# Zero-column matmuls on TensorE ahead of the wait for each channel's exponentials

## What is computed

```
cos_pm = jnp.cos(phase_modulators)                # [channel, head]
for wl in range(16):
    m = cos_pm[wl][None, :, None, None]
    scores = einsum('bhqd,bhkd->bhqk', Q * m, K * m) * SCALE
    scores = scores * jnp.cos(KERR * scores * scores)
    attn = jax.nn.softmax(scores, axis=-1)
    acc += einsum('bhqk,bhkd->bhqd', attn, V) * interference_weights[wl]
x = _layernorm(x + (acc / 16) @ Wo + bo)
x = _layernorm(x + ffn(x))
```

## Time and profile before

| | us |
|---|---|
| median of 3 runs | 3671.42 (3670.53 to 3673.81) |
| the profiled execution itself | 3674.77 |
| span of that execution, first to last instruction | 3672.7 |
| ACT busy | 3476.3 (95%) |
| DVE busy | 2934.6 (80%) |
| PE busy | 2688.7 (73%) |
| mean granted TensorE clock | 0.882 of full |

### The profile page before, as it was taken

How to read it: one execution, slowest core, us unless ns; L and a number is a source line. 1 busy time by engine, 2 the same in 40 slices (tenths; PEclk the granted TensorE clock), 3 DMA queues, 4 the chain that set the end, 5 groups by cost and what they waited for, 6 DMA issues and landing times.

```text
span 3672.7 us, 50238 instructions
## 1 busy us (share of the span) xinstructions
PE 2688.7 (73%) x19639; PEld 823.7 (22%) x19639; DVE 2934.6 (80%) x3858; ACT 3476.3 (95%) x635; POOL 55.8 (2%) x206
## 2 busy tenths in 40 slices
PE   5777777777777777777777777777777777777673
PEld 2222222222222222222222222222222222222222
DVE  6788777788777788777788888788888888888787
ACT  6999999999999999999999999999999999999971
POOL 0000000000000000000000000000000000000000
PEclk7988988888889889888889898889888888988986
DMA  1000000000000000000000000000000000000000
GB/s 46 1 1 1 1 1 1 1 1 1 1 1 1 1 1 1 1 14 1 1 2 1 4 2 4 2 4 1 2 4 2 4 2 1 4 2 4 2 26 29
DMA packets 19221, 16.65 MB, mean 5 GB/s; under 512 B 4177, under 2 KB 16866, under 8 KB 18722
## 3 DMA queue, kind: packets, MB, share of 16 engines
q1 hardware_dynamic: 18130, 12.54, 1.2%
q10 hardware_dynamic: 720, 0.34, 0.0%
q0 software_dynamic: 128, 0.26, 0.0%
HBM read 7.76 MB, written 5.37 MB: 4 GB/s over the span
## 4 chain that ended last, share of the span: by engine, by line
ACT 53%; issue 27%; PE 9%; DVE 4%; ACTq 4%; DMA 0%; POOL 0%; DVEq 0%; POOLq 0%
ACT probs L597 53%; PE psum L1200 7%; ACTq L590 3%; DVE x_p L668 1%; PE psum L719 1%; DVE m_pad L770 0%; ACTq L594 0%; DVE x_p L686 0%; DVE probs L843 0%; PE psum L699 0%; DVE probs L1106 0%; DVE q_s L654 0%; DVE q_t L762 0%; ACT probs L614 0%; DVE k_s L654 0%
## 5 line engine op out<-in xcount | busy, mean ns | idle before, releaser
L597 ACT ACTIVATE probs<-s_t 128x8192 f32<-128x8192 f32 (+1 forms) x512 | 3440.8, 6807 | 69.2 <-PE psum L1200 67.6
L1200 PE MATMUL psum<-probs,v_pad 128*27 128x512 f32 x15872 | 2239.1, 691 | 578.7 <-ACT probs L597 523.0
L1200 PEld LDWEIGHTS psum<-probs,v_pad 128*27 128x27 f32 x15872 | 568.4, 119 | 1976.5 <-issue 1382.2
L668 DVE SCALAR_TENSOR_TENSOR x_p<-x_p,x_y 128x1024 f32<-128x1024 f32 x640 | 782.0, 1222 | 14.2
L1385 DVE COPY o_sb<-psum 128x512 f32<-128x512 f32 x192 | 132.7, 691 | 249.9 <-PE psum L1200 237.5
L791 DVE COPY s_t<-psum 128x2048 f32<-128x2048 f32 x130 | 297.0, 2284 | 11.2 <-PE psum L749 10.2
L770 DVE TENSOR_REDUCE m_pad<-psum 128x4 f32<-128x2048 f32 x132 | 301.6, 2286 | 3.9
L699 PE MATMUL psum<-x_p,v_pad 128*27 128x512 f32 x512 | 157.1, 696 | 190.1 <-DVE x_p L686 190.1
L761 DVE TENSOR_SCALAR v_t<-psum,b_head 128x512 f32<-128x512 f32 x33 | 24.8, 751 | 208.1 <-PE psum L719 208.1
L686 DVE SCALAR_TENSOR_TENSOR x_p<-x_p,x_2k 128x1024 f32<-128x1024 f32 x128 | 156.8, 1225 | 4.4
L1184 PE MATMUL psum<-ident,o_sb 128*128 128x128 f32 x768 | 122.1, 282 | 47.9 <-DVE weighted L1373 47.9
(11 more groups left out here) (244 smaller groups left out, 990.8 us busy)
## 6 DMA issues: line engine op xcount, KB each, us to landing
x_next_dram<-weighted SPq DMA_DIRECT2D x1, 1024.0 KB, 3.9
x_group<-x_next_dram SPq DMA_DIRECT2D x1, 1024.0 KB, 4.9
loop_memory<-in_L_attn_x_dram SPq DMA_DIRECT2D x8, 128.0 KB, 2.1
x_dram<-loop_memory SPq DMA_DIRECT2D x8, 128.0 KB, 1.8
out_dram<-loop_memory SPq DMA_DIRECT2D x8, 128.0 KB, 1.8
x_dram<-probs SPq DMA_DIRECT2D x2, 512.0 KB, 3.6
out_dram<-probs SPq DMA_DIRECT2D x2, 512.0 KB, 3.6
s_t<-in_L_ffn_ew_dram SPq DMA_DIRECT2D x3, 256.0 KB
```

Of the source, the lines that this page charges most:

```text
L597: nc.scalar.activation(probs[:, w % 2, n0:], s_t[:, p, n0:], ACT.Exp, scale=scales[w % 2]).then_inc(s["exp_done"], 1)
L668: link(nc.vector.scalar_tensor_tensor(out=x_p[:], in0=x_p[:], scalar=c, in1=x_y[:], op0=ALU.add, op1=ALU.mult))
L1200: last = nc.tensor.matmul(products_of(wg)[L * b:L * b + SLOTS * A, :], v_pad[:, p, b * T + kt, c0:c0 + SLOTS * A], probs[:, w % 2, at:at + ...
```

## The change

A helper `spin_pe` is added. In each step but steps 2 and 7 it issues 2 rounds, that is 8 matmuls, whose stationary operand is 18 columns of `v_pad` that hold zeros and whose moving operand is 512 columns of `s_t`. They write to rows of the bank that the step's product accumulates into. In the first step of a group but the last they carry start and stop flags, so that they write zeros, which the product's first matmul replaces; in the others they add zeros. The wait for `exp_done` moves behind them; the wait for `o_copied` (a bank's last contents have been copied) now stands ahead of them.

```diff
+SPINS = 2
+SPIN_STEPS = tuple(w for w in range(W) if w not in (2, 7))
...
+        def spin_pe(w, wg, p):
+
+            for r in range(SPINS if w in SPIN_STEPS else 0):
+                for b in range(NB):
+                    nc.tensor.matmul(products_of(wg)[L * b:L * b + VPAD, :], v_pad[:, p, b * T, 0:VPAD],
+                                     s_t[:, p, b * S:(b + 1) * S], start=(w in FIRST_OF and w < W - 1), stop=(w in FIRST_OF and w < W - 1))
+
...
                             for w in range(W):
                                 if w in PRODUCT_STEPS:
                                     piece_pe(pe, PRODUCT_STEPS[w], u, p)
-                                pe.wait_ge(s["exp_done"], u * W + (w + 1))
                                 if w in FIRST_OF:
 
                                     wg = FIRST_OF[w]
                                     pe.wait_ge(s["o_copied"], u * NWG + (wg + 1))
+                                spin_pe(w, wg, p)
+                                pe.wait_ge(s["exp_done"], u * W + (w + 1))
```

## The result

| | before | after |
|---|---|---|
| median, us | 3672.61 (4 runs) | 3793.03 (4 runs, 3792.14 to 3793.81) |
| ratio, 95% interval | | 1.0313 (1.0288 to 1.0338) |
| span of the profiled execution, us | 3672.7 | 3790.6 |
| mean granted TensorE clock | 0.882 | 0.938 |
| ACT waits for products, us in all (times) | 67.6 (43) | 178.2 (93) |

What follows compares the result with a forecast made beforehand. ACT, busy 95% of the span, was taken as the bound. Back edges (+5.27 us, 14 times: 73.8) and other passages (+0.99, 17 times: 16.8) gave +90.6 on 3671.4: 3762.0 us; range 3648 to 3810, the forecast's own 3710 to 3800.

Steps and rivals of the forecast that it cites:

- The gain: Ahead of step 0: step 14's product at full clock lets ACT start 1.50 us earlier at each of 31 passages.
- Step 0 behind a back edge: After PE's branch, added rounds delay step 0's product, so ACT waits at step 2: 3.07 us lost, half clock included.
- Step 4: Rounds behind the late piece delay exponential 6: 2.49 us lost with half clock, 3.70 us behind a back edge.
- Steps 8 and 11: Same order of piece and rounds costs up to 1.71 us, but ACT has room; counted as zero.
- That zero columns hold the clock: Assumption at the added rounds: matmuls of zeros raise the clock as much as a product's round does.
- The rival that they do nothing: Zero columns do not hold the clock, so 1.50 us stay lost and delays come: 3808.5 us, chance 0.08.
- Rivals 3 and 4: 3: back edge not felt, clock holds, 3649.7 us, chance 0.11; 4: only the gain, step 4 free, 3624.9 us, chance 0.09.
- rivals 1 and 2: 1: full clock everywhere, 3685.8 us, chance 0.10; 2: half clock at the back edge only, 3709.5 us, chance 0.13.
- rival 6: Whole kernel: gains and delays cancel within 0.2%, about 7 us; chance 0.07.

Runs made afterwards that it cites:

- e4: The change with all its rounds, but in steps 4, 8, 11 and 15 placed ahead of the piece's wait instead of behind it: 3674.7 us.
- e9: The change with rounds in steps 4 and 14 only, those of step 4 behind the piece's wait as in the change: 3670.2 us.
- e10: The change with rounds in steps 4 and 14 only, those of step 4 ahead of the piece's wait: 3624.2 us.
- e3: The change without its rounds in steps 0 and 15: 3742.4 us.
- e7: The change with rounds in steps 0 and 14 only: 3665.3 us.
- e8: The change with rounds in steps 14 and 15 only: 3675.1 us.
- e6: The change with rounds in step 14 alone, and one round there instead of two: 3670.0 us.
- e1: The change with its two rounds in step 14 alone: 3637.1 us.

## Why the prediction came out as it did

**The direction and the reason were right.** The forecast said slower, with new gaps of ACT ahead of step 6 in nearly all units and ahead of step 2 in every second one, and half clock behind the branch and around the piece. All of it is in the trace after: gaps ahead of step 6 in all 32 units, and ahead of step 2 in the first unit and the 14 behind a back edge. e4 and e9 with e10 show that it is the place behind the piece's wait; e3, e7 and e8 show that rounds on either side of the branch cost time. The size came out low: 3793 us lies inside the forecast's own range of 3710 to 3800, near its top, and the reason given for that top, a longer slow stretch, is a part of what happened.

**The gain** was put at 1.50 us at each of 31 passages. 24 passages have a gap of 0.25 or 0.26 us, a gain of 1.52. The 7 back edges of the second loop kept 1.47 to 1.49 us. The miss is 7 x 1.2, about 8.5 us. There the rounds behind the piece of step 11 and PE's feed-forward work in steps 12 and 13 add up until the product of step 14 starts 1.3 us late; I had set the cost of steps 8 and 11 at zero and counted feed-forward work nowhere. In e4, whose rounds in steps 8 and 11 stand ahead, all 31 gaps are 0.26 us or less. Step 14's products kept full clock, in the first loop behind 1.52 to 1.57 us of idle, as forecast; but the ground given for it, that 1.73 us had kept the clock in the rows of before, was not a safe one, since 1.66 us in the same trace had not (under e6).

**Step 0 behind a back edge** was put at 3.07 us; the gaps are 3.4 to 3.9 us. With the 0.10 us of lost overlap that is some 0.6 us more, a fifth. I took one stretch of half clock like those of the earlier trace rows, on the rounds alone. The trace after has half clock from 1635.8 to 1642.5 around the branch, twice as long: it sets in while PE idles and stays when the rounds start, so they run at half clock from their first column to their last, and the product behind them still takes 3.98 us instead of 3.64. That is about half of the 0.6 us; the rest is that PE reaches the rounds later, 10.14 us after the unit's first exponential starts (1638.43 - 1628.29) where the forecast had 9.78. The branch itself is as before (a median of 3.48 us against 3.46 in the earlier trace rows). The added 14 x 0.6 us are some 8 us. The Trainium skill (Runtime: NRT & Kernel Launch, section "Instruction fetch mechanics") says that a taken branch to code that is no longer loaded waits for a fetch by DMA. The trace fits, since the same loop's branch takes 3.3 to 3.9 us on PE when it goes back and 0.08 us when it falls through, but no run here shows the fetch as the cause.

**Step 4** was put at 2.49 us and, behind a back edge, at 3.70. Measured, with the 0.10 us of lost overlap: 3.74 behind back edges, as forecast. The others split: 2.06 to 2.29 in the first loop, 3.66 to 4.03 in the second. Of the first loop's 2.1 us, 0.8 are the rounds (e9) and the rest half clock on a part of the work (in the windows above, 1553.9 to 1557.2; the piece starts at 1554.50). In the second loop's units within an iteration the piece comes another half microsecond later, and half clock lasts twice as long. The window around the piece of such a unit (columns as above):

```profile
2458.40:2465.10 6.70, 5.38 (x28) 0.50 0.01 2
```

and the piece in PE's timeline:

```profile
2459.72 1.06 PE L701 MATMUL psum<-x_p,v_pad 128*27 128x512 f32 x2 [2.56 <-DVE x_p L688]
```

In sum the gaps ahead of step 6 grew by 96.1 us (105.0 against 8.9 before) where some 94 were forecast. That they agree so well is luck: with the lost overlap, the 8 units of the first loop are some 3 us below the forecast together, the 9 of the second some 13 above it, and the very first unit, which the forecast leaves out, has 3.6 us.

**Steps 8 and 11** were put at zero. Step 8's product costs 4 us of gaps ahead of step 10; step 11's share is in the 8.5 us above.

**That zero columns hold the clock**, which the trace of before could not show, is shown: step 14 at full clock in all units, 1.00 in its window. The rival that they do nothing (3808.5) lies close to the measured time, but its mark, products of over 5 us in step 14, is absent. By the time alone it would have been nearer than the forecast. Rivals 3 and 4, the faster ones, fall by the gaps at steps 2 and 6; rivals 1 and 2 (full clock everywhere, or at the piece) by the windows at 0.50; rival 6 by the time.

In sum, ACT's gaps after are 111 us more than before: 39 less ahead of step 0 (46.5 were forecast), 50 more ahead of step 2 (43), 96 more ahead of step 6 (94) and 4 more ahead of step 10 (none). The span grew by 118; the remaining 7 us are, for the most part, the overlap of 0.10 us that each of some 50 additional interruptions costs.

## What to carry to other kernels

Matmuls that only hold the clock belong into time in which the engine would otherwise wait, and so ahead of the wait that ends last, not merely ahead of some wait: in an in-order queue everything behind an earlier wait, or behind a branch that the engine is late from, is paid in full. Count for each place how long the engine idles behind the last instruction that it can already run; where a piece or a branch comes first, that time is gone when the filler starts. And look at the next wait: in e8 a product that came later and ran faster lengthened the idle time ahead of the next one, and the half clock moved there. One place out of sixteen gave about two thirds of the gain that any run showed (3637 us), two gave 3624, and fourteen lost 120 us.

## What had not been expected of the hardware

- An idle time of 2.43 us ahead of a product was followed by half clock in 13 of 16 units and by full clock in 3, with the same instructions around it (e6). Over the products of steps 0 to 14 in all twelve traces, those behind 1.35 to 3.29 us of idle met either level: 670 were at full clock throughout, 856 were slowed. Ahead of step 14, 1.52 to 1.58 us never was followed by half clock (16 units of the first loop in e1, and 16 in the changed kernel).
- Half clock that sets in during an idle time can last twice as long as in the earlier trace rows when work resumes within it (1635.8 to 1642.5, and 2458.4 to 2465.1), and rounds of zeros that start then run at half speed: 3.62 instead of 1.9 us.
